# Masked attention, first batch: the mask enters the scores on TensorE, and VectorE takes plain maxima

## The reference, cut to what matters

```
q = split_heads(layernorm(x) @ Wq + bq);  k = split_heads(ctx @ Wk + bk);  v = split_heads(ctx @ Wv + bv)
logits = einsum('bhqd,bhkd->bhqk', q, k) / sqrt(8)
logits = logits + mask.astype(float32) * -1e9        # mask: (8, 1, 256, 256) of 0 and 1
attn = softmax(logits, axis=-1)
x = x + einsum('bhqk,bhkd->bhqd', attn, v) @ Wo + bo
```

## Time and profile before

| | us |
|---|---|
| median of 3 runs | 516.68 (515.92 to 517.56) |
| profiled execution, its own time | 516.38 |
| its span, first to last instruction | 514.6 |
| TensorE busy | 448.6 (87%) |
| VectorE busy | 355.0 (69%) |
| ScalarE busy | 302.4 (59%) |
| GpSimd busy | 217.9 (42%) |
| mean granted clock of TensorE | 0.951 of full speed |

### The profile page before, as it was taken

The page is one execution under the profiler, slowest core; times in us unless marked ns, Lnnn a source line. Parts: engine busy times, 40 slices in busy tenths (PEclk is TensorE's granted clock), DMA queues, the critical chain, the costliest instruction groups (busy, mean ns, idle before and its releaser), DMA issues.

```text
span 514.6 us, 11513 instructions
## 1 busy us (share of the span) xinstructions
PE 448.6 (87%) x3693; PEld 366.9 (71%) x3693; DVE 355.0 (69%) x1297; ACT 302.4 (59%) x649; POOL 217.9 (42%) x439
## 2 busy tenths in 40 slices
PE   3669999999997879966999999999999799899960
PEld 2467767777775668854777778788777589799960
DVE  6767787878783288878787787877878258444424
ACT  5237777767767468873266666557566545466540
POOL 4660364123316135555101225454453557666650
PEclk9989999999999999977599999999999979999995
DMA  7463324332405994043243334433310301323107
GB/s 216 148 215 100 102 79 132 100 99 76 135 4 226 426 421 171 0 134 97 80 116 126 114 100 138 132 107 113 110 60 3 85 23 32 86 80 86 53 15 245
DMA packets 40699, 61.56 MB, mean 120 GB/s; under 512 B 6121, under 2 KB 30506, under 8 KB 39232
## 3 DMA queue, kind: packets, MB, share of 16 engines
q1 hardware_dynamic: 38080, 56.20, 33.8%
q0 software_dynamic: 2272, 4.24, 2.6%
q10 hardware_dynamic: 288, 0.39, 0.2%
HBM read 31.45 MB, written 29.23 MB: 118 GB/s over the span
## 4 chain that ended last, share of the span: by engine, by line
PE 46%; DVE 12%; issue 5%; ACT 3%; DMA 2%; POOL 1%; DVEq 0%; POOLq 0%; SPq 0%; ACTq 0%
PE ps L1677 6%; PE ps L1868 6%; PE ps L1637 6%; PE ps L1719 6%; PE ps L1879 5%; PE ps L1722 5%; DVE ps L1278 2%; ACT probs L1007 2%; PE ps L1846 1%; DMA k_blocks<-y_dram 1%; DVE fa L1487 1%; PE ps L1933 1%; DVE conv_out L908 1%; PE ps L1620 1%; PE ps L1604 1%
## 5 line engine op out<-in xcount | busy, mean ns | idle before, releaser
L1007 ACT ACTIVATE probs<-ps 128x512 f32<-128x512 f32 x256 | 147.3, 598 | 85.0 <-PE ps L1722 80.7
L1637 PE MATMUL ps<-k_blocks,q_stacks 128*128 128x256 f32 x512 | 123.2, 326 | 12.7 <-DVE row_max L1278 4.5
L1278 DVE CUSTOM_DVE_ANT_0 ps<-ps,mask_q 128x256 f32<-128x256 f32 x256 | 102.6, 450 | 23.5 <-PE ps L1637 21.5
L1722 PE MATMUL ps<-q_stacks,k_blocks 128*128 128x256 f32 x512 | 106.6, 292 | 1.9 <-DMA q_stacks<-maxT 1.8
L1722 PEld LDWEIGHTS ps<-q_stacks,k_blocks 128*128 128x128 f32 x512 | 88.7, 193 | 21.9 <-issue 10.6
L1302 DVE TENSOR_REDUCE row_max<-ps 128x2 f32<-128x512 f32 x128 | 84.5, 686 | 26.6 <-PE ps L1637 25.3
L1637 PEld LDWEIGHTS ps<-k_blocks,q_stacks 128*128 128x128 f32 x512 | 84.4, 205 | 22.1 <-issue 8.7
L1677 PE MATMUL ps<-probs,v_aug 128*32 128x256 f32 x1024 | 69.2, 387 | 4.3 <-ACT probs L1007 3.1
L803 POOL TENSOR_SCALAR max_split<-row_max 128x16 fp32r<-128x16 f32 x32 | 6.6, 206 | 130.5 <-issue 87.0
L1719 PE MATMUL ps<-mask_k,neg_mask_eye 128*128 128x512 f32 x128 | 55.3, 432 | 0.0
L739 POOL DMA_INDIRECT y_dram<-x_ring x39 | 39.7, 1018 | 21.5 <-ACT x_ring L1086 12.7
(11 more groups left out here) (214 smaller groups left out, 748.4 us busy)
## 6 DMA issues: line engine op xcount, KB each, us to landing
slots_dram<-x_ring SPq DMA_DIRECT2D x1, 10400.0 KB, 30.0
q_stacks<-q_dram SPq DMA_DIRECT2D x32, 256.0 KB
k_blocks<-k_dram SPq DMA_DIRECT2D x128, 48.0 KB
q_dram<-qk_parts SPq DMA_DIRECT2D x16, 256.0 KB, 2.9
k_dram<-qk_parts SPq DMA_DIRECT2D x16, 256.0 KB, 2.9
mask_in<-host_mask SPq DMA_DIRECT2D x8, 512.0 KB, 3.6
experts<-host_experts SPq DMA_DIRECT2D x1, 4096.0 KB, 39.0
x_ring<-slots_dram SPq DMA_DIRECT2D x39, 65.0 KB, 2.1
```

The costliest lines, as they stand in the source:

```text
L1007: eng.activation(probs[:, n // HPS % 2, n % HPS, :, :].rearrange("p k q -> p (k q)"), ps[:, head_bank(BANKS_T, n)[0], :], ACT.Exp).then_in ...
L1278: last = eng.tensor_tensor_reduce(out=scored, in0=scored, in1=mask_q[t % 2][:, i, :], scale=1.0, scalar=-3.0e38, op0=ALU.add, op1=ALU.max, ...
L1637: mm = eng.matmul(ps[:, bank, i * S:(i + 1) * S], q_stack[r][:, st, i * P:(i + 1) * P], k_blocks[r][:, st, j, :], start=True, stop=True)
L1722: mm = eng.matmul(ps[:, bank, k * S:(k + 1) * S], k_blocks[r][:, st, j, k * P:(k + 1) * P], q_stack[r][:, st, :], start=(l == 0), stop=(l ...
```

## The change

In batch 0 of the masked layer alone, `scores` starts each head's bank with a product of `neg_mask_eye` by a mask tile that has the queries on the partitions, and the two score products add to it. `plain_max` then takes the maximum with one `tensor_reduce`, as in the first layer. The tile used is `mask_k[2]`, which GpSimd writes at b = -2 in place of `mask_q[0]`. All other batches stay as they were.

```diff
@@ attention_gpsimd, body
-                    eng.tensor_scalar(mask_q[r][:, :, :], mask_in[:, 0, :, :], -MASK_A * MASK_B, 1.0,
-                                      ALU.mult, ALU.mult).then_inc(a.k_q, 1)
+                    if b == -2:
+                        eng.tensor_scalar(mask_k[2][:, :, :], mask_in[:, 0, :, :], MASK_B, 1.0,
+                                          ALU.mult, ALU.mult).then_inc(a.k_q, 1)
+                    else:
+                        eng.tensor_scalar(mask_q[r][:, :, :], mask_in[:, 0, :, :], -MASK_A * MASK_B, 1.0,
+                                          ALU.mult, ALU.mult).then_inc(a.k_q, 1)
@@ vector
+        def plain_max(eng, a, t, n):
+
+            eng.wait_ge(a.s_ps, t * 16 + n + 1)
+            eng.tensor_reduce(row_max[:, :, n], ps[:, head_bank(BANKS_S, n)[0], :].rearrange("p (i k) -> p i k", i=NT),
+                              AX.X, ALU.max).then_inc(a.s_max, 1)
+
         def masked_max(eng, t, n):
 
             a = att[1]
+            if t == 0:
+                plain_max(eng, a, t, n)
+                return
             if n == 0:
                 hold(eng, a.k_q, t + 1)
             hold(eng, a.s_ps, t * 16 + n + 1)
@@ scores
+            masked = l == 1 and isinstance(b, int) and b == 0
+            if masked:
+                if n == 0:
+                    eng.wait_ge(a.k_q, 1)
+                eng.matmul(ps[:, bank, :], neg_mask_eye[:, :], mask_k[2][:, :, :].rearrange("p i k -> p (i k)"),
+                           start=True, stop=False)
             for i in range(NT):
                 mm = eng.matmul(ps[:, bank, i * S:(i + 1) * S], q_stack[r][:, st, i * P:(i + 1) * P],
-                                k_blocks[r][:, st, j, :], start=True, stop=True)
+                                k_blocks[r][:, st, j, :], start=not masked, stop=not masked or i == NT - 1)
             mm.then_inc(a.s_ps, 1)
```

More of the change, by code:

```diff
@@ L1300, in body @@
                         if l == 0:
-                            eng.wait_ge(a.s_ps, (b + 1) * 16 + n + 1)
-                            eng.tensor_reduce(row_max[:, :, n], ps[:, head_bank(BANKS_S, n)[0], :].rearrange("p (i k) -> p i k", i=NT),
-                                              AX.X, ALU.max).then_inc(a.s_max, 1)
+                            plain_max(eng, a, b + 1, n)
                         else:
```

## The result

Over 22 executions of each kernel, the changed kernel takes 513.57 us in the median (510.84 to 515.93) and the kernel before 516.16 (512.01 to 517.97). The ratio is 0.9958, 95% interval 0.994 to 0.9977: faster, by 2.2 to 2.6 us. The profiled execution of the changed kernel took 514.34 us (span 512.6, mean granted clock 0.967), against 516.38 (514.6, 0.951) before.

The account below looks back on a forecast made before the run. It took the two-bank loop up to 250.38 us, then TensorE at half clock to 255.6, to set the end. Front -0.2, low heads +0.16, cover +0.5, high-clock steps -0.94, body -2.0: -2.5, median 514.2 us, range 512.6 to 517.0.

Parts of the forecast that it names:

- stage: From first value products of the first layer's last batch to those of masked batch 0; the forecast's summed -2.5 us.
- front to head 6: Batch 0's front part, heads 0 to 3 before batch 7's residual: shorter maxima on VectorE save 0.2 us.
- heads 6 to 15, cover included: Batch 0's two-bank loop: four low-clock heads +0.16, lost idle time on TensorE +0.5, six high-clock steps -0.94 us.
- cover: TensorE's idle time hiding work between heads; its loss charged 0.8 us at low clock, 0.5 if half low, 0.2 if high.
- body, batch 1's heads 0 to 4: Start of batch 0's body, then at half clock, runs at full clock: -2.0 us (bounds 1.2 and 2.6).
- seven bodies behind: Untouched bodies after the stage, up to batch 7's value products; the prediction had no term for them.
- Rival D: Heads end earlier but batch 0's body does not follow, waiting for loaded maxima: -1.0, 515.7 us; chance 0.18.
- The clock's turns: TensorE in batch 0's heads: added products raise the clock near 245 to 246 us, not at 255.6.
- rival B: Clock never falls at 238.7 us, so all ten loop steps run at high clock: -3.6, 513.1 us; chance 0.26.
- The loop's turn: Two heads of batch 0's scores, maximum, scores over two banks: 1.62 us at high clock, 2.01 at low.
- Rival C: Clock stays low until the body's dense products, so the loop only lengthens: +1.0, 517.7 us; chance 0.14.

Follow-up runs that it names:

- second pair: The kernel before and the changed kernel, unaltered, each profiled once more; between these two profiles the stage again differs by 3.85 us.
- products_only: Kernel before plus one 512-column product a head in batch 0, overwritten by the scores, VectorE's masked maxima kept; 513.96 us.
- plain_only: Changed kernel without its 16 products, mask left out of batch 0's maxima, which are plain reductions; 513.86 us.
- front_heads: Kernel before with the change for heads 0 to 5 of batch 0 only, GpSimd writing both mask tiles; 513.50 us.
- fills_before: Kernel before plus 23 products nobody reads, where TensorE waits ahead of and between heads 0 to 3; 512.06 us, ratio 0.9938.
- plain_fills: Changed kernel without its 16 products, mask left out of batch 0's maxima, plus 23 unread filling products; 511.18 us, ratio 0.9914.
- products_look: One more profiled execution of products_only, no further change; its stage took 96.77 us.
- hold_clock: Changed kernel plus unread filling products, 5 before head 2's scores and 4 before head 3's; 512.91 us.
- four_fills: Changed kernel plus 23 fills, 30 short products ahead of the first layer's batch 0 and 9 before row transposes near 410 us; 1.9 us faster than before.
- two_fills: Changed kernel plus the 23 filling products near 221 to 236 us; 510.56 us, ratio 0.9918.
- back_heads: Kernel before with the change for heads 6 to 15 of batch 0 only, GpSimd writing both mask tiles; 512.42 us.

## Why the prediction was right, and where it was not

The forecast was 514.2 us, 2.5 below the kernel before; it came out at 513.57, with 2.2 to 2.6 below. That the two differences agree so well is partly luck: the stage gained 1.1 us more than forecast, and 0.76 were given back elsewhere. The steps:

| step | forecast, us | measured, us |
|---|---|---|
| front to head 6 | -0.2 | -0.4 (241.49 - 241.59, less 0.3 of the prologue) |
| heads 6 to 15, cover included | -0.3 (+0.16 + 0.5 - 0.94) | -1.3 (9.75 to 8.46) |
| body, batch 1's heads 0 to 4 | -2.0 | -1.9 (6.09 to 4.18) |
| stage | -2.5 | -3.6, and -3.85 in the second pair |
| seven bodies behind | 0 | +0.76, and +0.64 in the second pair |

**The body** went as forecast, and products_only and plain_only show why: 4.2 us with the high clock under either kind of maximum in batch 0, 5.43 with the clock low until 251.9 (of which the body lies under 3.0 us, against 4.5 before). Rival D is out: the first shifted product starts at 249.6, and the loaded maxima were not what it waited for.

**The clock's turns** were the step that failed, though the outcome survived it. I had it fall at 238.7 and rise near 245, so that four heads went at the low clock. It fell at 236.0 and rose at 239.4, and all ten heads of the loop went at the high one. That is rival B's sum in full (-0.2 - 1.6 + 0.2 - 2.0 = -3.6), reached without B's condition, since the clock did fall. I had argued the rise from work exceeding what the low clock can do. TensorE's busy time doesn't bear this out as a rule: it was busy 2.25 of 2.60 us ahead of the rise at 239.4, but 6.54 of 7.40 in plain_only (243 to 250.4), and there the clock stayed low. What the profiles do show is where it turned: with products or fills at these heads no low stretch is longer than 6.8 us, without them it is 17.1 us (the kernel before, plain_only) or 20.5. Why it rises when it does stays open.

**The loop's turn** at the high clock was forecast at 1.62 us and is 1.53 to 1.59 (heads 12 to 14, 9 to 11). In the chain the added products take 0.28 to 0.50 us each there, the longest after a wait. *The Trainium skill, "TensorE: Matmul & The Clock Gate", "Back-to-back issue gap", has 131 ns for 512 columns; no run here came near it.*

**The cover** was charged 0.5 us, or 0.2 at the high clock. What it is can be seen in the chain of the changed kernel (start, length, what):

```profile
243.90 0.62 POOL mask_q L769
244.52 0.08 issue
244.61 0.62 POOL mask_k L773
...
245.31 0.21 POOL max_split L807
...
245.96 0.40 PE ps L1631 x4
...
246.91 0.70 DVE row_max L1277
```

The faster heads reach the transposes of the maxima before GpSimd has split them, because two mask tiles stand ahead of the split in its queue. TensorE waits 0.34 us there, a new wait that I had not named.

**Rival C** (clock low, slower) did not come. Its page's rule, *"A second HAM failure mode: psum-queue depth-cycling" in the same page of the Trainium skill*, would have the loop over two banks lose the clock again and again. Here the loop kept 1.00 from 239.4 us on, through TensorE's pauses of 0.28 to 0.35 us for a maximum or the split. But the same loop without products did lose it in all three profiles that had the high clock behind its first heads: front_heads at 246.6 us, fills_before at 242.8, plain_fills at 243.7. Of the eight profiles with products in heads 6 to 15 only products_look fell there, at the loop's first head (240.3), and from 244.7 us on all eight read 1.00 up to the body. So a loss of the clock, as the rule has it, does happen in this loop without the products; they seem to hold the clock there as well as to bring it back, on one profile of most kernels.

**The 0.76 us given back** were in no term. They come in two jumps of 0.4 us, in the body of batch 3 (near 324 us) and that of batch 7 (just ahead of the mark at 397). VectorE at the first one, in the changed kernel, and a like row in front_heads:

```profile
323.62 0.43 DVE L1291 CUSTOM_DVE_ANT_0 ps<-ps,mask_q 128x256 f32<-128x256 f32 x1 [0.31 <-issue]
```

```profile
342.22 0.43 DVE L1293 CUSTOM_DVE_ANT_0 ps<-ps,mask_q 128x256 f32<-128x256 f32 x1 [0.34 <-issue]
```

"issue" is idle time for which the profile shows no cause. All kernels with 16 plain maxima lose it (this stage is 142.2 to 142.4 us in the change twice, plain_only, plain_fills, hold_clock, four_fills and two_fills, and 141.5 to 141.75 in the others), whether TensorE has products added or not. And at the same instruction: plain_only has a row like the first at 323.80, two_fills one at 318.83. front_heads, which takes fewer instructions from VectorE (18 instead of 48), has it elsewhere, at a cost in this stage of 0.1; back_heads (30 fewer) has no such row between 254 and 402 us. products_only, at the high clock, has no such row either. So it goes with VectorE's program and not with the clock. That it is the arrival of that engine's instructions, and hangs on where in the stream a wait falls, is argued only; no run tested it.

**How sure is the size?** Between executions of one kernel the time falls with the mean granted clock: by 2.6 us for each 0.01 before (29 executions, correlation -0.75), by 2.4 after (22, -0.76). But that is no price for a given stretch. In the other kernels the slope lies anywhere from 0.4 (plain_only, -0.19) to 6.3 us (four_fills, -0.90), and in two_fills it even has the other sign. The median clock goes from 0.954 (those 29) to 0.970 with the change, which by the two slopes would be 3.7 to 4.0 us, more than came. The ledger of the stage, 3.6 less 0.76, gives 2.9, near the medians' 2.6.

## What to carry to other kernels

- Before you price an engine's work, look at what its clock is granted in that stretch and what it did just before each turn. Work added to TensorE in a loop that waits for another engine can pay for itself when it brings the high clock back and work bound by TensorE follows. The body, which nobody had touched, got 1.9 us shorter; the products alone, their own time paid, saved 1.1 to 1.8.
- Products that nobody reads, put where TensorE waits anyway, are a cheap test of whether the clock is the cause: 23 of them gained 0.6% in the kernel before. They must not delay work that is ready: 30 short ones in the prologue held up the first layer by some 3 us.
- Look at the clock in the whole of a stage before you compare it between profiles. A low stretch of 3.4 us ahead of any change made single gains look like 0.05 and 0.7 us where they were 1.7 and 2.3, and so made two separate gains look as if they needed each other.
- A faster loop meets the next queue: look for what stands ahead of its consumer's inputs on GpSimd.

## What the runs showed of the hardware that was not expected

- The clock's turns vary between executions of one kernel. At 236 to 239 us the fall moved by 2.3 us, and the prologue's turns move the first layer's start by 3.7 us (38.8 to 42.5), with the same instructions there in all kernels but four_fills. A low stretch that starts between 186 and 191 us is there in 5 of 14 profiles and costs 1.6 us. One profile's span can't be compared with another's within 4 us; a stage between two marks can, within some 0.2 us, where the clock's turns between them agree.
- In a loop over two banks the clock, once high, fell again in three profiles of three without the added products, and in one of eight with them.
- The same product of 512 columns takes 0.23 to 0.37 us behind another product and up to 0.50 after a wait, at the high clock; four fills in a row took 1.17 us, with the first at 0.39 at least 0.26 for each further one.
